# First tile's expert up projections made during the quantised attention, and eight groups ahead of the gates

## The reference

```
# block 5: cross attention with fake quantised operands, 16 heads of width 16
q, k, v = fq_sym(q * scale), fq_sym(k), fq_sym(v)
attn = softmax(einsum('bhqd,bhkd->bhqk', q, k))
attn = fq_unsigned(attn)                 # 1024 keys, 8 bits
out  = einsum('bhqk,bhkd->bhqd', attn, v) @ Wp + bp
# block 6: 64 experts of hidden width 32, top 6 of sigmoid scores, capacity 128
shared = silu(g_s) * y_s @ w_shared_down
up = einsum('ecd,edh->ech', x_disp, w_up); g_r, v_r = split(up)
out_r = einsum('ech,ehd->ecd', silu(g_r) * v_r, w_down)
```

## Time and profile before

| | |
|---|---|
| median of 3 runs | 448.67 us (448.04 to 448.78) |
| the profiled execution | 446.82 us, of which the span is 445.0 us |
| busy share of the span | PE 83%, DVE 68%, ACT 48%, PEld 49%, POOL 25% |
| mean granted TensorE clock | 0.926 of full speed |
| exponentials of the 64 units | start at 234.57 to 335.88 us |
| block 6, from the last tile's transposed copy to the last matmul | 346.8 to 436.5 us |

### The profile page before, as it was taken

How to read it: one execution, slowest core, us unless ns; L and a number is a source line. 1 busy time by engine, 2 the same in 40 slices (tenths; PEclk the granted TensorE clock), 3 DMA queues, 4 the chain that set the end, 5 groups by cost and what they waited for, 6 DMA issues and landing times.

```text
span 445.0 us, 6798 instructions
## 1 busy us (share of the span) xinstructions
PE 369.6 (83%) x2355; PEld 219.1 (49%) x2379; DVE 304.7 (68%) x636; ACT 211.5 (48%) x540; POOL 110.5 (25%) x214
## 2 busy tenths in 40 slices
PE   5978859599987999989976657778669897999993
PEld 2535547444443566657753323335337444556662
DVE  3896988989624587889779888998993652222335
ACT  2781412462245665765526758988985420111100
POOL 8237778648471000000111101211120000000002
PEclk9998996889999599999989886896998999999997
DMA  8994111850000000020026789997998004122111
GB/s 255 292 371 91 1 3 2 330 236 1 0 1 0 1 2 1 1 49 0 4 47 104 143 156 157 159 159 144 161 174 233 3 5 149 40 55 47 49 47 47
DMA packets 81857, 41.42 MB, mean 93 GB/s; under 512 B 70496, under 2 KB 77600, under 8 KB 81376
## 3 DMA queue, kind: packets, MB, share of 16 engines
q1 hardware_dynamic: 79520, 40.93, 38.2%
q0 software_dynamic: 2304, 0.07, 1.5%
HBM read 21.58 MB, written 2.88 MB: 55 GB/s over the span
## 4 chain that ended last, share of the span: by engine, by line
PE 55%; DVE 14%; DMA 10%; issue 9%; POOL 6%; ACT 6%; SPq 0%; POOLq 0%; DVEq 0%; ACTq 0%
PE ps L798 28%; PE ps L1254 6%; DMA area_b<-area_a 6%; PE ps L1037 5%; PE ps L1048 4%; POOL deltas L508 4%; DVE area_a L1629 3%; ACT area_a L724 3%; PE ps L970 2%; PE ps L1031 2%; PE ps L1098 2%; ACT area_a L699 2%; DMA area_b<-deltas 2%; DMA deltas<-entry_w,small 1%; DVE stats L1374 1%
## 5 line engine op out<-in xcount | busy, mean ns | idle before, releaser
L1629 DVE CUSTOM_DVE_ANT_0 area_a<-ps,zero,small 128x1024 f32<-128x1024 f32 x64 | 79.5, 1274 | 7.8 <-PE ps L1098 3.8
L724 ACT ACTIVATE area_a<-area_a,small 128x1024 int16<-128x1024 f32 x64 | 73.1, 1143 | 22.6 <-POOL small L563 13.7
L699 ACT ACTIVATE area_a<-ps,small 128x256 f32<-128x256 f32 (+1 forms) x128 | 52.0, 430 | 31.8 <-DVE small L1571 28.0
L798 PE MATMUL ps<-xT_odd,early 128*128 128x512 f32 (+2 forms) x136 | 58.3, 571 | 0.9 <-DVE area_b L1711 0.8
L486 POOL TENSOR_SCALAR var_eps<-meanvar 128x1 f32<-128x1 f32 x24 | 7.0, 293 | 198.5 <-DVE meanvar L1375 198.3
L1711 DVE TENSOR_TENSOR area_b<-ps,area_b 128x512 f32<-128x512 f32 x16 | 11.0, 690 | 50.5 <-ACT area_b L773 50.5
L1571 DVE TENSOR_REDUCE small<-ps 128x4 f32<-128x1024 f32 (+1 forms) x24 | 29.3, 1222 | 20.2 <-PE ps L1037 17.3
L773 ACT ACTIVATE area_b<-ps 128x512 f32<-128x512 f32 x16 | 9.5, 596 | 61.9 <-PE ps L798 61.9
L798 PEld LDWEIGHTS ps<-xT_odd,early 128*128 128x128 f32 x136 | 24.9, 190 | 26.3 <-issue 22.3
L798 PE MATMUL ps<-area_b,xT_even 128*128 128x512 f32 x64 | 31.4, 637 | 5.2 <-ACT area_b L676 5.2
L563 POOL TENSOR_SCALAR small<-small 128x1 f32<-128x1 f32 x64 | 12.7, 198 | 84.5 <-DVE small L1629 84.4
(11 more groups left out here) (278 smaller groups left out, 637.9 us busy)
## 6 DMA issues: line engine op xcount, KB each, us to landing
early<-in_w_up_dram SPq DMA_DIRECT2D x1, 4096.0 KB, 13.5
area_b<-gates_out SPq DMA_DIRECT2D x16, 256.0 KB, 3.1
deltas<-area_b SPq DMA_DIRECT2D x1, 2112.0 KB, 17.7
area_b<-deltas SPq DMA_DIRECT2D x2, 1024.0 KB, 5.8
area_a<-in_w_down_dram SPq DMA_DIRECT2D x1, 2048.0 KB, 11.5
early<-in_ctxT_dram SPq DMA_DIRECT2D x1, 1024.0 KB, 13.1
early<-in_ctx_dram SPq DMA_DIRECT2D x1, 1024.0 KB
area_b<-area_a SPq DMA_TRANSPOSE x59, 3.3
```

Source lines behind the costliest of these rows:

```text
L699: a = act.activation(p1[:, n % 2, x * nk * P:(x + 1) * nk * P], scores1(n)[:, x * nk * P:(x + 1) * nk * P], ACT.Exp, bias=nmx1[:, n % 2, x ...
L724: act.activation(px[:, u % PX, :], sx[:, u % 3, :], ACT.Exp, bias=nbx[:, u:u + 1], accum_out=zx[:, i, h:h + 1]).then_inc(sem("px_ready"), 1)
L798: mm = pe.matmul(dst, lhsT(c), rhs(c), start=start and c == 0, stop=stop and c == DC - 1, **kw)
L1629: dve.tensor_tensor_reduce(sx[:, u % 3, :], bank(2 * (u % 2), 2), zero[:].broadcast_to([P, B * M]), qsc[:, i, h:h + 1], LOWEST, ALU.add, A ...
```

## The change

- A new constant `FOLD` names groups 2 to 15, and `FOLD_AT` is 31. PE transposes tile 0 for block 6 already in iteration 31 of block 5, into bank 5, and ACT copies it out after the exponential of unit 33.
- In iterations 33, 35, ... 59 PE makes the up projection of one of these groups for tile 0 alone (`fold`: four matmuls of 128 columns, bank 5, columns 0 to 255). It waits for the copy of the fold before. ACT copies the raw result to `first_up` after the exponentials of units 36, 38, ... 62.
- Since bank 5 is taken, PE's transposes of units use bank 4 alone, except unit 63.
- In block 6 the up projection, silu and gate product of groups 2 to 15 take 384 tokens. For tile 0, ACT makes silu of seven groups at once after silu(2) and of the other seven after silu(3) (`silu_first`), and DVE multiplies them around gate(5) (`gate_first`). `hidden` becomes two products for these groups.
- `AHEAD` is 8: up(6) and up(7) are made ahead of down(0), and gate(6) ahead of hidden(0).
- `w_down` lies where block 5's buffers are, so its load waits for all 64 exponentials; `gate_rows` moves in its area.

```diff
-AHEAD = 6
+AHEAD = 8
+FOLD_AT = HX + NORM_AT + 1
+FOLD = tuple(range(2, NG))
+        first_up = carve("a", 8 * N + D, [len(FOLD), 2, P])
+        def folded(u):
+            k = u - FOLD_AT - 2
+            return k // 2 if k >= 0 and k % 2 == 0 and k // 2 < len(FOLD) else None
+        def begins(g):
+            return P if g in FOLD else 0
@@ SP, ahead of the load of w_down @@
+                sp.wait_ge(sem("px_ready"), TT * HX)
@@ ACT, stage5, after evac_px of unit u @@
+                    if u == FOLD_AT + 2:
+                        act.wait_ge(sem("xT_ps"), nth(5, 0))
+                        act.activation(xT[1][:, :, 0:P], bank(5)[:, 0:D]..., ACT.Copy)
+                    if folded(u - 3) is not None:
+                        k = folded(u - 3)
+                        act.wait_ge(sem("first_up_ps"), k + 1)
+                        act.activation(first_up[:, k]..., bank(5)[:, 0:D], ACT.Copy).then_inc(sem("first_up_out"), 1)
@@ ACT, stage6 @@
+                def silu_first(half):
+                    act.wait_ge(sem("first_up_out"), len(FOLD))
+                    a = first_up[:, half * len(FOLD) // 2:(half + 1) * len(FOLD) // 2, 0, :]
+                    act.activation(a, a, ACT.Silu).then_inc(sem("silu_first_ready"), 1)
                 for g in range(4):
                     silu_of(g)
+                    if g >= 2:
+                        silu_first(g - 2)
@@ PE, stage5, after turn(u - 1) @@
+                def fold(k):
+                    if k:
+                        pe.wait_ge(sem("first_up_out"), k)
+                    else:
+                        pe.wait_ge(sem("in_w_up"), 16)
+                        pe.wait_ge(sem("xT_ready"), nth(5, 0))
+                    rows = slice(P * FOLD[k], P * (FOLD[k] + 1))
+                    for m in range(2):
+                        mm = dense(bank(5)[:, m * P:(m + 1) * P], lambda c: w_up[:, c, m, rows], tile_of(5, 0))
+                    mm.then_inc(sem("first_up_ps"), 1)
+                    if folded(u) is not None:
+                        fold(folded(u))
@@ PE, stage6 @@
-                    up_part(g, slice((TT - 1) * P if g == 0 else 0, N)).then_inc(sem("up_ps"), 1)
+                    up_part(g, slice((TT - 1) * P if g == 0 else begins(g), N)).then_inc(sem("up_ps"), 1)
-                up(5)
+                for g in range(5, AHEAD):
+                    up(g)
@@ DVE, stage6 @@
+                gate_first(0)
                 gate(5)
-                dve.wait_ge(sem("gated_ready"), AHEAD)
+                gate_first(1)
+                gate(6)
...
+                    if g in FOLD:
+                        TTN(out=hidden[:, s, 0:P], in0=gate_rows[:, g % 4, 0:P], in1=first_up[:, FOLD.index(g), 0, :], op=ALU.mult)
+                    own = slice(begins(g), N)
+                    TTN(out=hidden[:, s, own], in0=gate_rows[:, g % 4, own], in1=gated[:, g % AHEAD, own], op=ALU.mult)
```

More of the change, by code:

```diff
@@ L237, in build @@
         w_up = carve("early", 0, [DC, 2, E1 * HE])
-        w_down = carve("a", 4096, [NG, D])
+        w_down = carve("a", 0, [NG, D])
+        first_up = carve("a", 8 * N + D, [len(FOLD), 2, P])
         gate1T = carve("b", 0, [N], rows=E1)
@@ L241, in build @@
         gated = carve("b", 18 * N, [AHEAD, N])
-        gate_rows = carve("b", 24 * N, [4, N])
+        gate_rows = carve("b", 14 * N, [4, N])
         gates_out = nc.dram_tensor("gates_out", (E1, N), F32).ap()
@@ L283, in unit5, with turn_bank @@
             return u // HX, HEADS[u % HX]
+        def turn_bank(u):
+            return bank(5 if u == TT * HX - 1 else 4)
+        def folded(u):
[3 more added lines that the diff above has]
+            return P if g in FOLD else 0
         def before5(u, by_act):
@@ L727, in stage5 @@
                         evac_px(u - 2)
+                    if u == FOLD_AT + 2:
+                        act.wait_ge(sem("xT_ps"), nth(5, 0))
+                        act.activation(xT[1][:, :, 0:P], bank(5)[:, 0:D].rearrange("p (c t) -> p c t", c=DC), ACT.Copy).then_inc(sem("xT_ready"), 1)
+                    if folded(u - 3) is not None:
+                        k = folded(u - 3)
+                        act.wait_ge(sem("first_up_ps"), k + 1)
+                        act.activation(first_up[:, k].rearrange("p m t -> p (m t)"), bank(5)[:, 0:D], ACT.Copy).then_inc(sem("first_up_out"), 1)
                     if u == AT_3 - 1:
@@ L745, in evac_px @@
                 pTx_free(act, u)
-                act.activation(pTx[u % PT], bank(4 + n % 2).bitcast(I16), ACT.Copy).then_inc(sem("pTx_act"), 1)
+                act.activation(pTx[u % PT], turn_bank(u).bitcast(I16), ACT.Copy).then_inc(sem("pTx_act"), 1)
             def evac_sums(i):
@@ L772, in silu_of @@
                         act.wait_ge(sem("gated_ready"), g - 1)
-                    act.activation(silu[:, g % 2, :], bank(g % 2), ACT.Silu).then_inc(sem("silu_ready"), 1)
+                    own = slice(begins(g), N)
+                    act.activation(silu[:, g % 2, own], bank(g % 2)[:, own], ACT.Silu).then_inc(sem("silu_ready"), 1)
+                def silu_first(half):
+                    act.wait_ge(sem("first_up_out"), len(FOLD))
+                    a = first_up[:, half * len(FOLD) // 2:(half + 1) * len(FOLD) // 2, 0, :]
+                    act.activation(a, a, ACT.Silu).then_inc(sem("silu_first_ready"), 1)
                 for g in range(4):
                     silu_of(g)
+                    if g >= 2:
+                        silu_first(g - 2)
                 act.wait_ge(sem("gate1T_ps"), 1)
@@ L1104, in turn @@
                     pe.wait_ge(sem("px_ready"), u + 1)
-                    if n > 2:
-                        pe.wait_ge(sem("pTx_act"), n - 2)
+                    if u == units - 1:
+                        pe.wait_ge(sem("first_up_out"), len(FOLD))
+                    elif n > 1:
+                        pe.wait_ge(sem("pTx_act"), n - 1)
                     for k in range(KT):
-                        mm = pe.transpose(bank(4 + n % 2).bitcast(BF16)[:, k * P:(k + 1) * P],
+                        mm = pe.transpose(turn_bank(u).bitcast(BF16)[:, k * P:(k + 1) * P],
                                           px[:, u % PX, k * P:(k + 1) * P].bitcast(BF16), ident_b[:])
@@ L1169, in stage5 @@
                         turn(u - 1)
+                    if u == FOLD_AT:
+                        pe.wait_ge(sem("x_ready"), nth(5, 0))
+                        for c in range(DC):
+                            mm = pe.transpose(bank(5)[:, c * P:(c + 1) * P], x_tok[1][:, 0, c * P:(c + 1) * P], ident[:])
+                        mm.then_inc(sem("xT_ps"), 1)
+                    if folded(u) is not None:
+                        fold(folded(u))
                     if u > HX and u % HX == 5:
@@ L1197, in stage5 @@
                         pe.wait_ge(sem("maxx_ready"), units - 1)
-                        for i in range(TT - 1):
+                        for i in range(1, TT - 1):
                             pe.wait_ge(sem("x_ready"), nth(5, i))
@@ L1204, in stage5 @@
                 project(TT - 1)
-                pe.wait_ge(sem("in_w_up"), 16)
                 up_part(0, slice(0, (TT - 1) * P))
@@ L1679, in stage5 @@
                             norm_scale(5, i)
-                for i in range(TT - 1):
-                    dve.wait_ge(sem("xT_ps"), nth(5, max(i, 1)))
+                for i in range(1, TT - 1):
+                    dve.wait_ge(sem("xT_ps"), nth(5, i))
                     slot = bank(i // 2)[:, D * (i % 2):D * (i % 2) + D].rearrange("p (c t) -> p c t", c=DC)
@@ L1710, in gate, with gate_first @@
                     dve.wait_ge(sem("silu_ready"), g + 1)
-                    TTN(out=gated[:, g % AHEAD, :], in0=bank(2 + g % 2), in1=silu[:, g % 2, :], op=ALU.mult).then_inc(sem("gated_ready"), 1)
+                    own = slice(begins(g), N)
+                    TTN(out=gated[:, g % AHEAD, own], in0=bank(2 + g % 2)[:, own], in1=silu[:, g % 2, own],
+                        op=ALU.mult).then_inc(sem("gated_ready"), 1)
+                def gate_first(half):
+                    mine = slice(half * len(FOLD) // 2, (half + 1) * len(FOLD) // 2)
+                    dve.wait_ge(sem("silu_first_ready"), half + 1)
+                    TTN(out=first_up[:, mine, 0, :], in0=first_up[:, mine, 1, :], in1=first_up[:, mine, 0, :],
+                        op=ALU.mult).then_inc(sem("gated_first"), 1)
                 for i in range(TT):
@@ L1729, in stage6 @@
                 TTN(out=shared, in0=bank(4)[0:HS, :], in1=silu_shared, op=ALU.mult).then_inc(sem("shared_ready"), 1)
+                gate_first(0)
                 gate(5)
-                dve.wait_ge(sem("gated_ready"), AHEAD)
+                gate_first(1)
+                gate(6)
                 for g in range(NG):
                     s = g % 2
-                    if g >= AHEAD:
-                        dve.wait_ge(sem("gated_ready"), g + 1)
+                    dve.wait_ge(sem("gated_ready"), g + 1)
+                    if g in FOLD:
```

(11 more changed lines are left out.)

## The result

The changed kernel takes 443.46 us (median of 20 runs), the kernel before 447.29 us in as many runs beside it: ratio 0.9921, 95% interval 0.9896 to 0.9946. That is 3.5 us less (2.4 to 4.7); the forecast was 3.3 less. The profiled execution took 444.74 us, with a span of 443.0. Some executions are slow, by 1.5 to 3 per cent, and the ratios leave them out; two of the profiled ones are among them, this one and that of the kernel with folds and six groups ahead.

A forecast was written before the change was run, and what follows sets the result against it. PE alone was taken to bound the expert stage, no single engine the attention stage. Expert stage -13.3 and attention stage +10.0 gave -3.3 us on 448.67: 445.3 us, range 440.0 to 451.5.

The forecast's parts named there:

- Expert stage: Block 6, groups 2 to 15 with 384 columns instead of 512 and two more made ahead of down(0): 13.3 us less.
- allowance of 0.3: End of the expert stage: gate(15) between hidden(8) and hidden(9) on DVE, about 2.0 us against 1.73 of cover: 0.3 us more.
- The walk: Attention stage, queues followed unit by unit from 34 to 63 at the forecast prices: exp(63) at 346.6 against 335.88, +10.7 us.
- waits at turn_z: Attention units 38 and 54: ACT waits for turn_z standing behind a fold on PE, 1.44 us each, +2.9 us.
- Scalar turns: Attention units 40, 49 and 58: turns behind PE's late queue, ACT idling 1.8, about 1.1 and 0.9 us, +2.3 us.
- Waits for late scores: Attention units 45 to 51, 59, 60 and 63: ACT held up because scores come late, +5.4 us.
- DMA wait of 0.4: Attention stage: one wait for DMA, 0.4 us.
- The copy: ACT in the attention stage: 0.28 us per 256-column copy, fifteen copies 4.2 us (3.8 to 5.7).
- The tail: After exp(63): one transpose pair fewer and turn(62) long done, so the last apply follows after 3.4 us, not 4.1: -0.7 us.
- (b): Rival, attention stage: PE waits before folds and drops to 1.2 GHz, so the kernel is slower, middle 451 us; chance 0.20.
- (a): Rival, attention stage: PE keeps up, ACT pays its copies (4.2) and perhaps 1 us more, net -9, 440 us; chance 0.24.
- (c): Rival: gain cancels through dearer copies, folds at 1.1 us or 1 us less from the expert stage, 448.5 us; chance 0.14.

The follow-up runs named there:

- the second profile: The changed kernel profiled again with nothing edited, beside the other kernels on the same chip: ratio 0.9892 (0.985 to 0.993) against the kernel before.

## Why the prediction was right, step by step

- **Expert stage, -13.3: measured -13.73.** down(0) stands 25.97 us after the last copy in the chain, 25.67 by my table, 25.60 before, and hidden(0) is done some 0.8 us ahead of it, as forecast. From down(0) to the residual 50.0 instead of 64.1 us. The allowance of 0.3 near the end was not needed: down(9) follows 0.2 us after down(8).
- **The walk, +10.7 at exp(63): measured +12.45**, 11.55 of it from unit 36 on, 10.22 in the second profile, which begins at 295.72. The stretch is 51.99 and 50.66 us, forecast at about 51, and from exp(63) to the residual it is 14.4 and 13.0 us shorter than before, forecast at 12 to 14. Predicted waits at turn_z 1.44 each, measured 1.36 twice, in both profiles. Scalar turns 1.8, 1.1 and 0.9: measured 1.70, 0.99 and 0.44 in the second profile. In the first, turn(40) came 3.03 late, with PE's clock at 0.65. Waits for late scores 5.4: measured 5.2 and 5.1, at units 45, 46, 49, 59, 60 and 63, all of them on the list; the DMA wait of 0.4 did not come. A fold took 1.09 us to the next PE instruction (305.08 to 306.17), 0.97 by price. The terms of order in the sum are 2.9 + 2.3 + 5.4 + 0.4 = 11.0; moving the copy took 11.0 us away from the first profile and 9.7 from the second.
- **The copy, 0.28 us: 0.27** (297.47 to 297.74). The rule of the Trainium skill that the prediction set beside it ("ScalarE: Activation LUTs", Rules for kernel authors) gives its 0.3 us for an ACTIVATE whose bias is read through a pointer. This copy reads nothing but `ps` in the trace, so the estimate of 0.51 us was made with a rule that is not for it; the measured spacing and the record of 0.37 decide.
- **The tail, -0.7:** -0.69 in the first profile. In the second it was +0.76, with the clock at 0.85.
- **Rivals.** (b), the clock, is seen in its beginnings: 0.65 over 4 us in one profile, 0.85 over the tail in the other, worth 1.3 and 1.4 us, not the 3.3. It weighs more when the waits get longer, as with the later copy. (a) is false for this kernel and true for its neighbour: with the copy a unit earlier PE keeps up, and then even (a) was too dear, since I had added 4.2 us of copies and 1 us besides; the stretch grew by 0.55. Here the sum was not well built: the copies were entered as work (+3.9) and the old idling as taken back (-4.4), and only their sum, near nothing, has a meaning. My expectation for the earlier copy used the first without the second and missed by 4 us. (c) did not come; its causes, dearer folds and copies and a late hidden(0), were absent.

The forecast on time, 3.3 less against 3.5 (2.4 to 4.7), is within what the measurement can tell (0.25% to either side, where I had put 0.2%). The mechanism is borne out, the closeness is partly luck: by stages the forecast was off by 0.4 us one way (the expert stage) and by 1.8 the other (the attention stage, +10.0 against 12.45 - 0.69), and the profiled spans, forecast to be 3.3 shorter, are 2.0 and 2.5 shorter. The absolute time, 445.3 us, was 1.8 too high, 1.4 of it because three runs had put the kernel before at 448.67 and twenty put it at 447.29.

What stays open: why the medians differ by 3.8 us and the profiled spans by 2.0 and 2.5, and which 1.2 us the kernel with eight ahead and no folds lost in the attention stage (ACT's waits for DMA and POOL there are 4.7 us where they were 2.5).

## What to carry to other kernels

Work put into an engine's idle time costs first of all the waits that it brings, and only then its length. Here the same 14 folds and copies cost 11.6 us (10.2 in the second profile) with the copy after the third unit and 0.6 with it after the second. So ask of a moved piece what stands behind its wait in the same queue, follow that chain back to the engine where it began, and divide by how many units it may span; if the result is near the pace of the loop, move the release a unit earlier before anything else. And pieces made shorter ahead of a fixed latency leave a longer gap there unless their number is raised as well: PE idled 2.86 us ahead of down(0) with the shorter groups and six ahead, 2.23 with the longer ones, and not at all with eight.

## What I had not expected of the hardware

- After an idle time of 2.86 us ahead of down(0) its eight records took 3.65 us instead of 1.89, with a granted clock of 0.58 from 386 to 390. In the kernel before, 2.23 us of idling in the same place left down(0) at 1.96 us. Each is one execution, the first 7.5 us above the median of its kernel.
- With PE's idle time filled, its clock over the attention stretch was 1.00 in the kernel with the earlier copy (PE busy 38.42 of 41.00 us), where both profiles without folds have 0.90 (29.73 of 41.00 in the kernel before). So part of the added work was paid for by work that was there running faster.
- The same kernel had its low clock in different places: 0.65 at turn(40) in one execution, 0.85 after exp(63) in the other, for nearly the same loss. Ahead of turn(40) PE had done the same in both, with the same gap of 1.36 us ahead of the fold, and ran the apply behind it in 1.04 us in one and in 0.62 in the other.
- A chain across engines that leaves PE waiting can be slowed by the clock as well: with the later copy, waits of up to 3.1 us for a copy went with a mean clock of 0.73 and with folds of 2.07 us instead of 1.16.
